# The third layer's update in one stage: turning, gated update and next projection joined

## What is computed

```python
for _ in range(N_STEPS):                       # 4
    trans = jnp.einsum('nd,tod->tno', h, W_edge) + b_edge[:, None, :]
    msg = trans[etypes, src]
    a = jax.ops.segment_sum(msg, dst, num_segments=N)
    h = _gru_cell(a, h, W_ih, W_hh, b_ih, b_hh)
# _gru_cell: r = sigmoid(ir + hr); z = sigmoid(iz + hz)
#            n = tanh(inn + r * hn); h = (1 - z) * n + z * h
```

## Time and profile before

| | us |
|---|---|
| runs of before, median of 3 | 12100.61 (12093.36 to 12107.19) |
| the profiled execution, its own time | 12019.95 |
| its span, first to last instruction | 12018.1 |
| mean granted TensorE clock in it | 0.734 of full |

### The profile page before, as it was taken

How to read it: one execution, slowest core, us unless ns; L and a number is a source line. 1 busy time by engine, 2 the same in 40 slices (tenths; PEclk the granted TensorE clock), 3 DMA queues, 4 the chain that set the end, 5 groups by cost and what they waited for, 6 DMA issues and landing times. The chain is left out here.

```text
span 12018.1 us, 148393 instructions
## 1 busy us (share of the span) xinstructions
PE 6550.1 (55%) x36272; PEld 5479.0 (46%) x36273; DVE 4612.7 (38%) x10118; ACT 2251.5 (19%) x4313; POOL 6209.6 (52%) x6365
## 2 busy tenths in 40 slices
PE   3666786566786665884335334433533443365555
PEld 3555665555765555853323223233323322244443
DVE  4444754444754444752113112211311221135555
ACT  1222552222542222641000000000000000011111
POOL 2666423666414665504663665466366456625553
PEclk6777898777897777996667666666766666677777
DMA  2444322444313443401111111211111121112221
GB/s 75 128 127 127 103 64 69 128 127 125 106 42 88 129 128 105 125 22 42 46 45 61 46 46 36 68 45 46 60 45 45 34 71 46 46 43 77 78 77 55
DMA packets 698434, 894.29 MB, mean 74 GB/s; under 512 B 148417, under 2 KB 443211, under 8 KB 698130
## 3 DMA queue, kind: packets, MB, share of 16 engines
q0 software_dynamic: 198368, 429.61, 13.6%
q1 hardware_dynamic: 498474, 461.96, 12.4%
q10 hardware_dynamic: 1416, 0.86, 0.0%
HBM read 698.72 MB, written 193.14 MB: 74 GB/s over the span
## 5 line engine op out<-in xcount | busy, mean ns | idle before, releaser
L857 POOL DMA_INDIRECT states<-table_typed,tile_idx x2512 | 2415.9, 962 | 1777.8 <-issue 721.2
L840 POOL DMA_INDIRECT states<-table_x,src_idx x2016 | 1980.1, 982 | 1862.7 <-POOLq L82 742.8
L979 PE MATMUL psum<-states,l_sums_select 128*128 x4480 | 905.5, 336 | 1729.7 <-issue 1696.3
L979 PEld LDWEIGHTS psum<-states,l_sums_select 128*128 128x128 f32 x4480 | 777.0, 244 | 1854.3 <-issue 1853.8
L961 DVE SCALAR_TENSOR_TENSOR l_sums_select<-dst_all,pair_start,iota_row 128x512 f32<-128x512 f32 x560 | 402.1, 749 | 2212.5 <-remote 1401.0
L1091 PE MATMUL psum<-ident,select 128*128 128x128 f32 x2016 | 418.3, 344 | 1199.3 <-DVE states L1059 723.4
L840 POOL DMA_INDIRECT l_pass_ring<-table_kv,src_idx x672 | 655.1, 975 | 658.9 <-DVE score L1312 286.3
L1068 DVE TENSOR_TENSOR states<-w,psum 128x512 f32<-128x512 f32 x504 | 345.2, 685 | 1544.0 <-ACT w L1048 969.0
L857 POOL DMA_INDIRECT states<-table_x,tile_idx x628 | 602.1, 959 | 626.2 <-POOLq L82 337.0
L979 PE MATMUL psum<-states,select 128*128 x2240 | 469.4, 348 | 808.8 <-issue 769.4
L944 ACT COPY t<-psum 128x512 f32<-128x512 f32 x50 | 29.3, 585 | 4534.1 <-PE psum L979 2586.3
(11 more groups left out here) (357 smaller groups left out, 11997.4 us busy)
## 6 DMA issues: line engine op xcount, KB each, us to landing
states<-in_edge_attr_dram SPq DMA_DIRECT2D x2016, 64.0 KB
rows_dram<-l_scores_mixT SPq DMA_DIRECT2D x504, 256.0 KB
l_values_ring<-rows_dram SPq DMA_DIRECT2D x504, 256.0 KB
table_typed<-l_rows_rows SPq DMA_DIRECT2D x40, 1024.0 KB, 4.3
states<-table_typed,tile_idx POOLq DMA_INDIRECT x2512
states<-table_x,src_idx POOLq DMA_INDIRECT x2016
l_pass_ring<-table_kv,src_idx POOLq DMA_INDIRECT x672
table_x<-l_rows_rows SPq DMA_DIRECT2D x40, 256.0 KB, 2.3
```

What stands on the lines that cost most here:

```text
L840: pool.indirect_dma_start(out=ring[:, k % REGIONS, u, :], out_offset=None, in_=table, in_offset=at).then_inc(gathered[k % REGIONS], 16)
L857: pool.indirect_dma_start(out=ring[:, k % TILE_RING, u, :], out_offset=None, in_=table, in_offset=at).then_inc(gathered[k % REGIONS], 16)
L979: ins = pe.matmul(to, picked(k)[:, u, :], rows, start=False, stop=True, skip_group_check=True)
```

## The change

The third layer gets a new block, `gated_update`, that turns the sums, updates the states and, where a right-hand side is given, projects the new states for the next step. The first projection stands ahead of the loop, with an empty clearing block after it; the loop has three turns of `sum_pass` and `gated_update` with projection; the fourth pass and its update without projection stand behind the loop. The update's subtraction, product and addition go from VectorE to GpSimd. Turned sums are copied by ScalarE instead of VectorE, and the projection reads `hT` itself instead of a staged copy. The tiles lie in `states`, which the sums use as ring between updates. PSUM has one bank for turning, four for the gates (one set), three for the projection. The code is written out for the 10 chunks, with the order of the steps given by `waves`.

```diff
--- before.py
+++ after.py
@@ -1667,6 +1667,120 @@
                             dve.tensor_tensor(h[:, cols(c)], new[:, u, :], gate[:, u, 0, :], ALU.add).then_inc(g_step, 1)
                         pairs(dve, reset, update)
 
+        u_turned, u_copied, u_product, u_gated, u_reset, u_read, u_new, u_step, u_projected, u_kept = sems(
+            "sums_turned", "sums_copied", "gate_products", "gates_made", "reset_applied", "gate_banks_read", "new_made", "state_step",
+            "next_projected", "next_kept")
+
+        def gated_update(name, msg, h, w_ih, w_hh, gates, b_in, b_hn, rhs=None, bias=None, table=None):
+
+
+            room = states[:, 0:V * (4 + 4 * 4) * CHUNK // 2]
+            msgT = room[:, 0:V * CHUNK].rearrange("p (u f) -> p u f", u=V)
+            gate = room[:, V * CHUNK:3 * V * CHUNK].rearrange("p (u k f) -> p u k f", u=V, k=2)
+            new = room[:, 3 * V * CHUNK:4 * V * CHUNK].rearrange("p (u f) -> p u f", u=V)
+            rows = room[:, 4 * V * CHUNK:4 * V * CHUNK + V * 4 * CHUNK].rearrange("p (u k f) -> p u k f", u=V, k=4)
+            project = rhs is not None
+
+            def at(c):
+                return slice(c * CHUNK, (c + 1) * CHUNK)
+
+            def waves(*stages):
+
+                for t in range(CHUNKS + len(stages) - 1):
+                    for lag in reversed(range(len(stages))):
+                        if 0 <= t - lag < CHUNKS:
+                            stages[lag](t - lag)
+
+            with block(name, u_turned, u_copied, u_product, u_gated, u_reset, u_read, u_new, u_step, u_projected, u_kept, *r_stored) as b:
+                @b.tensor
+                def _(pe):
+                    def turn(c):
+                        at_least(pe, u_copied, c)
+                        for k in range(4):
+                            ins = pe.transpose(psum[:, 0, k * P:(k + 1) * P], msg[:, c * CHUNK + k * P:c * CHUNK + (k + 1) * P], ident[:])
+                        ins.then_inc(u_turned, 1)
+
+                    def gates_of(c):
+                        at_least(pe, u_gated, c)
+                        at_least(pe, u_read, c)
+                        pe.matmul(psum[:, 4, :], w_hh[2], h[:, at(c)], start=True, stop=True)
+                        for k in range(2):
+                            pe.matmul(psum[:, 1 + k, :], w_hh[k], h[:, at(c)], start=True, stop=False)
+                        pe.wait_ge(u_copied, c + 1)
+                        for k in range(2):
+                            pe.matmul(psum[:, 1 + k, :], w_ih[k], msgT[:, c % V, :], start=False, stop=True)
+                        pe.matmul(psum[:, 3, :], w_ih[2], msgT[:, c % V, :], start=True, stop=True).then_inc(u_product, 1)
+
+                    def next_rows(c):
+                        pe.wait_ge(u_step, 3 * c + 3)
+                        for k in range(4):
+                            at_least(pe, u_kept, 4 * c + k - 2)
+                            pe.matmul(psum[:, 5 + (4 * c + k) % 3, :], h[:, c * CHUNK + k * P:c * CHUNK + (k + 1) * P], rhs,
+                                      start=True, stop=True).then_inc(u_projected, 1)
+                    waves(*([turn, gates_of, next_rows] if project else [turn, gates_of]))
+
+                @b.scalar
+                def _(act):
+                    def copy(c):
+                        act.wait_ge(u_turned, c + 1)
+                        at_least(act, u_product, c + 1 - V)
+                        act.copy(msgT[:, c % V, :], psum[:, 0, :]).then_inc(u_copied, 1)
+
+                    def bend(c):
+                        act.wait_ge(u_product, c + 1)
+                        at_least(act, u_step, 3 * (c + 1 - V))
+                        act.activation(gate[:, c % V, 0, :], psum[:, 1, :], ACT.Sigmoid, bias=gates[:, 0:1])
+                        act.activation(gate[:, c % V, 1, :], psum[:, 2, :], ACT.Sigmoid, bias=gates[:, 1:2]).then_inc(u_gated, 1)
+                        act.wait_ge(u_read, c + 1)
+                        act.activation(new[:, c % V, :], new[:, c % V, :], ACT.Tanh, bias=b_in).then_inc(u_new, 1)
+                    waves(copy, bend)
+
+                @b.gpsimd
+                def _(pool):
+                    def update(c):
+                        pool.wait_ge(u_new, c + 1)
+                        pool.tensor_tensor(gate[:, c % V, 0, :], h[:, at(c)], new[:, c % V, :], ALU.subtract).then_inc(u_step, 1)
+                        pool.wait_ge(u_step, 3 * c + 1)
+                        pool.tensor_tensor(gate[:, c % V, 0, :], gate[:, c % V, 0, :], gate[:, c % V, 1, :], ALU.mult).then_inc(u_step, 1)
+                        pool.wait_ge(u_step, 3 * c + 2)
+                        pool.tensor_tensor(h[:, at(c)], new[:, c % V, :], gate[:, c % V, 0, :], ALU.add).then_inc(u_step, 1)
+
+                    waves(update)
+
+                @b.vector
+                def _(dve):
+                    def keep(c, k):
+                        dve.wait_ge(u_projected, 4 * c + k + 1)
+                        if c >= V:
+                            dve.wait_ge(r_stored[c % V], c // V * 16)
+                        dve.tensor_tensor(rows[:, c % V, k, :], psum[:, 5 + (4 * c + k) % 3, :], bias, ALU.add).then_inc(u_kept, 1)
+
+                    def reset(c):
+                        dve.wait_ge(u_gated, c + 1)
+                        dve.scalar_tensor_tensor(out=new[:, c % V, :], in0=psum[:, 4, :], scalar=b_hn, in1=gate[:, c % V, 0, :],
+                                                 op0=ALU.add, op1=ALU.mult).then_inc(u_reset, 1)
+                        dve.wait_ge(u_reset, c + 1)
+                        dve.tensor_tensor(new[:, c % V, :], new[:, c % V, :], psum[:, 3, :], ALU.add).then_inc(u_read, 1)
+
+                    for t in range(CHUNKS + 1):
+                        if project and t >= 1:
+                            keep(t - 1, 0)
+                            keep(t - 1, 1)
+                        if t < CHUNKS:
+                            reset(t)
+                        if project and t >= 1:
+                            keep(t - 1, 2)
+                            keep(t - 1, 3)
+
+                if project:
+                    @b.sync
+                    def _(sp):
+                        for c in range(CHUNKS):
+                            sp.wait_ge(u_kept, 4 * c + 4)
+                            sp.dma_start(table[at(c), :].rearrange("(b p) f -> p b f", p=P), rows[:, c % V, :, :]).then_inc(r_stored[c % V], 16)
+                        for stored in r_stored:
+                            sp.wait_ge(stored, 16 * (CHUNKS // V))
+
         b_stats, b_root, b_applied, b_scale, b_done = sems("bn_step", "bn_rooted", "bn_applied", "bn_product", "bn_done")
 
         def batch_norm(name, src, gain, shift, dst=None, residual=None, weight=None, bias=None):
@@ -1831,13 +1945,17 @@
                                (w3[:, 6:8, :], io["L3_gnn_W2"].rearrange("(k p) f -> p k f", p=P))):
                     sp.dma_start(to, of).then_inc(l_typed, 16)
                 sp.wait_ge(l_typed, 16 * 7)
-        with nc.Fori(0, L2_STEPS) as it:
-            projected_rows("l2_rows", hT, wt[:, WEDGE:WEDGE + 4, :].rearrange("p a b -> p (a b)"), 4 * D, table_typed, bias=bedge_rows[:])
-            sum_pass("l2_sums", table_typed.ap().rearrange("n (t f) -> (n t) f", f=D),
-                     [GAT_ITERS * ROWS + n + it * n for n in TILE_COUNTS], t1)
-            from_rows("l2_messages", t1, rows_in=t1)
-            gru("l2_gru", t1, hT, parts_of(wt, GGIH, 3), parts_of(wt, GGHH, 3), gate_bias[:, 1, :], wcol("2_b_ih", 2), wcol("2_b_hh", 2))
+        by_type = wt[:, WEDGE:WEDGE + 4, :].rearrange("p a b -> p (a b)")
+        typed_rows = table_typed.ap().rearrange("n (t f) -> (n t) f", f=D)
+        l2_gates = (parts_of(wt, GGIH, 3), parts_of(wt, GGHH, 3), gate_bias[:, 1, :], wcol("2_b_ih", 2), wcol("2_b_hh", 2))
+        projected_rows("l2_rows", hT, by_type, 4 * D, table_typed, bias=bedge_rows[:])
+        clear_block("l2_start")
+        with nc.Fori(0, L2_STEPS - 1) as it:
+            sum_pass("l2_sums", typed_rows, [GAT_ITERS * ROWS + n + it * n for n in TILE_COUNTS], t1)
+            gated_update("l2_update", t1, hT, *l2_gates, rhs=by_type, bias=bedge_rows[:], table=table_typed)
             clear_block("l2_end")
+        sum_pass("l2_last_sums", typed_rows, [GAT_ITERS * ROWS + L2_STEPS * n for n in TILE_COUNTS], t1)
+        gated_update("l2_last_update", t1, hT, *l2_gates)
         add_state("l2_residual", hT)
```

## The result

The changed kernel takes 12323.26 us, median of 4 runs (12318.02 to 12326.54), against 12097.06 for the kernel before (4 runs, 12093.36 to 12107.19): a ratio of 1.0184, 95% interval 1.0168 to 1.0200. That is 226 us slower, where 189 were forecast, inside the range that was given. The direction and the mechanism came out as said; 37 us are missing.

What follows compares the result with a forecast made beforehand. TensorE, running in written order, was taken to bound the update, with a chain now laid bare. Three looped stages +177.6, last update +10.1 and an added block +1.0 made +189 us on 12100.6: 12290 us, range 12225 to 12345.

Steps and rivals of the forecast that it cites:

- What bounds, and what is laid bare: Gated update: TensorE sets the pace, 53.85 of 62.00 us busy; the written order removes overlap between chunks.
- the whole chain: Joined stage, from a chunk's last gates matmul through its state update: 7.37 us, leaving TensorE idle near 6.9 us.
- The third rival, the hidden chain: Looped stages: TensorE does the next chunk's gates during the update; stage 108 us, time 12045 us; 4 in 100.
- Three GpSimd operations ... I take 1.04: State update on GpSimd: each operation 1.04 us, taken from the subtraction at L1144; 3.12 us per chunk.
- second rival: State update: GpSimd slower on two full tiles; at 1.5 us an operation 12333, at 2.08 12387; 12 in 100.
- I take 0.25, twice: State update: GpSimd waits for its own semaphore between its three operations, 0.25 us each time, 0.50 per chunk.
- The cold start, "I take 2.0": Looped stages: each TensorE burst after an idle 6.9 us starts at half clock and loses 2.0 us.
- The ends of a looped stage: Outside the nine periods: start 7.95 us, last chain and next_rows 12.8, last bias addition to first gather 7.35.
- I take none, since the gaps are near 2.4 us and the share of work is high: Last update: no clock loss in its gaps; period 8.0 us, stage 87.7 us.
- up to 18 us more: Last update: the added cost if the clock fell in its gaps too; in the range, not the sum.
- The rival that the clock would hold in the looped stages: Looped stages: turning in the gap keeps the clock up, no burst loses 2.0 us; time 12230; 8 in 100.
- Costed at nothing: Joined stage: bias additions, turned-sums copy and store run under other work, and VectorE does not slow GpSimd; 0 us.

Runs made afterwards that it cites:

- e1: The changed kernel with the order of lags in `waves` reversed, so next gates precede the wait for the state: 12012.36 us, 0.9997 of the kernel before.
- r0: Control: the changed kernel with only the semaphore values that four kinds of wait compare raised to at least 1: 12251.07 us, 1.0199 of the kernel before.
- e5: The changed kernel with GpSimd's subtraction given one broadcast input and its product replaced by a subtraction of two broadcasts, state not computed: 12259.94 us, one run.
- e4: The changed kernel with unused TensorE matmuls ahead of each turning but the first, filling the gap: 12195.57 us, 1.0152 of the kernel before.
- e3: The changed kernel, order kept, with the update's three operations back on VectorE: 12207.71 us, 1.0158 of the kernel before.
- e6: The changed kernel with the order reversed and the last update in the old separate turning and update stages: 11991.34 us, 0.9976 of the kernel before.
- e7: The changed kernel with order reversed, last update in its old stages, and the update's operations on VectorE: 11988.32 us, 0.9972 of the kernel before.
- e8: The kernel before, stages separate, with only the third layer's three update operations moved to GpSimd: 12034.57 us, 1.0012 of the kernel before.

## Why the prediction was right, and where it fell short

**What bounds, and what is laid bare: right.** TensorE set the pace before, runs its list in the written order, and stands at the head of `next_rows` for the whole chain. The third rival, the hidden chain, needed another order; e1 is that rival made true, with a period of 9.4 where its working said 9.1, and it takes 239 us away where r0 had lost 231. That rival's sum was too low all the same: its stage was 108 us and e1's are 115 to 118, and it put the time 55 us under before, where e1 is level. In one chunk of the trace of after it is 3.57 us from the gates' end to the tanh's end, forecast 3.57; this link was taken from rows of the same instructions.

**"Three GpSimd operations ... I take 1.04": too low.** They took 1.262 (second rival's direction, half its size):

```profile
L1742 POOL TENSOR_TENSOR states<-hT,states x40: 1260/1262/1274, 7552.5 to 10989.8; 128x512 f32<-128x512 f32 x40
```

Three are +0.67 us a chunk. e5 shows why: the row was of the right engine and size, but its inputs were two broadcasts. Its narrow spread said that the duration was firm, not that it applied. The Trainium skill's figure (GPSIMD Engine Reference, Performance versus the Vector engine), scaled to an estimate of 1.12 us, was nearer and also too low; the measurement decides.

**"I take 0.25, twice": too high.** The hand-over from one GpSimd operation to the next is 7571.88 - 7570.53 - 1.26 = 0.09, the next 0.07, and ScalarE to GpSimd 0.07 instead of 0.18. That gives back 0.45 of the 0.67. The chain is 7.64 instead of 7.37 us: two errors of opposite sign, and the near agreement is partly luck.

**The cold start, "I take 2.0": nearly.** All 30 bursts begin at 0.50. They rise by turns 3.2 to 3.5 and 5.1 to 5.8 us later (the windows of after have one of each); at half clock half of that is lost, 2.27 us in the mean. Every second period is therefore longer: 18.2 and 19.3, mean 18.7, where 17.94 was forecast. Of this 0.8 us the chain has 0.27 and the clock 0.27; 0.16 more is the time by which the last matmul of the gates outlasts its 0.86 us (1.02), which the sum left out. Nine periods make +7 us.

**The ends of a looped stage.** Its start took 6.1 us instead of 7.95, since the clock was still at 1.00 when the sums ended. From the gates of chunk 9 (end 7716.92) to the last bias addition's end it was 14.9 us instead of 13.5, and from there to the first gather 9.47 instead of 6.65:

```profile
7731.14 0.69 DVE L1756 TENSOR_TENSOR states<-psum,bedge_rows 128x512 f32<-128x512 f32 x1 [0.37 <-PE psum L1718]
...
7738.56 3.77 PE L982 MATMUL psum<-ones,blank 1*128 1x512 f32 x4 [7.46 <-PEq L82]
...
7741.30 0.98 POOL L857 DMA_INDIRECT states<-table_typed,tile_idx  x1 [16.80 <-issue]
```

In sum -1.8 + 7 + 1.4 + 2.8 = +9 us, and stage 1 is 198.54 against 189.6. Over the three stages +23 of the 38 that are missing. Of the last 2.8 us, 0.7 lie ahead of TensorE's first matmul of the sums (L982) and 2.1 between it and the first gather, 2.74 us instead of the 0.66 of before:

```profile
7599.05 13.99 PE L982 MATMUL psum<-ones,blank 1*128 1x512 f32 x16 [9.34 <-PEq L82]
...
7599.71 0.94 POOL L857 DMA_INDIRECT states<-table_typed,tile_idx  x1 [155.02 <-POOLq L82]
```

In turn 2 it is 3.10 us, in turn 3 only 0.45, and turn 3 is 3 us shorter than the others. Behind turns 1 and 2 the loop jumps back right ahead of the gathers, behind turn 3 it ends; in before the projection stood between. So this delay goes with the loop's turn; what in the turn costs it was not tried apart.

**"I take none, since the gaps are near 2.4 us and the share of work is high": this step failed.** In the last update the gaps are 2.5 us, as worked out, and the clock falls at their end or shortly behind all the same; the windows of the last update above show it. The period is 9.85 in the mean instead of 8.0, nine of them 16.6 us; the stage is 15.0 over its forecast of 87.7. e4 settles it: with the gap filled the same stage takes 89.1 us, 1.4 over. The prediction had the price ("up to 18 us more") and put it into the range. The only row on a gap was one of 5.96 us; no row showed that 2.5 was safe. The trace of before had gaps of this size too. In a score pass TensorE came back after 2.59 us, and eight matmuls of L1105 took 1.92 us soon after, where the next eight took 1.06:

```profile
818.99 0.66 PE L1091 MATMUL psum<-ident,select 128*128 128x128 f32 x4 [2.59 <-ACT l_scores_mixT L1040]
...
820.14 1.92 PE L1105 MATMUL psum<-wt,l_scores_mixT 128*128 128x128 f32 x8
...
824.23 1.06 PE L1105 MATMUL psum<-wt,l_scores_mixT 128*128 128x128 f32 x8
```

As in the last update, the burst began fast and the clock fell behind its start.

The Trainium skill (TensorE: Matmul & The Clock Gate, HAM oscillation) describes the pattern of the looped stages, short bursts with a wait between them, each starting cold; the trace agrees there, with 30 bursts of 30. The waits of that section's example are longer than the 2.5 us of the last update, where most bursts did not start cold but lost the clock within 1.3 us. The rival that the clock would hold in the looped stages is out: none of the 30 bursts began at full clock.

**Costed at nothing: held.** The bias additions, the copy on ScalarE and the store hide under the chain; the sums stayed at their 910 to 927 us. VectorE and GpSimd together show no slowing in the joined stage: L1742, which begins under two of VectorE's bias additions, took 1260 to 1274 ns, and L1744, behind them, 1260 to 1265.

**Where the 227 us of the stages come from.** The order accounts for all of them: reversed, 240 come back. Within the order of the change, GpSimd instead of VectorE is 56 of them and the clock at least 59. These overlap, since a shorter gap and a filled one act on the same wait, and they can't be added.

## What to carry to other kernels

Here the joined stages paid only in the order in which the consumer of chunk c stands behind the producer of chunk c+1 on the engine that works through its list; before joining, write the list down and see what lies between a product and the wait for it. The slower engine cost 43 us where its work lay bare (r0 against e3); covered, it cost nothing that shows (e6 against e7) or 14 us (e8), and since the engine that it relieved was not the bound, it brought nothing either. A duration is taken from a row with the same kinds of inputs, not only the same engine and size; and where a gap between bursts appears, the clock's price belongs in the sum until a row shows that such a gap is harmless; the trace of before is the place to look for gaps of that size.

## What the runs showed of the hardware

- With gaps of 2.5 us between bursts of some 7.5 us (the last update) TensorE's granted clock fell from 1.00 to 0.50 behind eight gaps of nine, mostly 0.2 to 1.3 us after the next burst had begun. With gaps of some 7.2 us (the looped stages) every burst began at 0.50 and came back after 3.2 to 3.5 or 5.1 to 5.8 us, by turns, so that equal chunks took 18.2 and 19.3 us. Where e4's matmuls left gaps of some 2 us, the clock held two times in three.
- A GpSimd operation on 128x512 fp32 took 1.26 us (1.28 in e8) with two full inputs, 1.26 with one, and 1.04 with both by broadcast; VectorE's was 0.69. GpSimd's next operation began 0.07 to 0.09 us after the one it waited for, although the one such wait in the trace of before was 0.25.
- In the trace of after the third layer's sums began 64 us later than in that of before, behind unchanged code; in the traces of the eight experiments they began at 5487.8 to 5498.6, beside the 5495.8 of before. Where the 64 us come from is not known. Two traces are therefore compared by stages and not by their spans.
